# 1444-key attention: the left-over maxima as two 64-row halves beside the scores, and the turn of the maxima as a 32-column product

## The reference, cut to what matters

```python
qm = _split_heads(q @ Wq.T + bq)      # 16 heads of 8
km = _split_heads(k @ Wk.T + bk)
vm = _split_heads(v @ Wv.T + bv)
scores = jnp.einsum('bnlh,bnph->bnlp', qm, km) / np.sqrt(HEAD_DIM)
scores = jnp.where(mask, scores, MASK_FILL)
attn = jax.nn.softmax(scores, axis=-1)
out = jnp.einsum('bnlp,bnph->bnlh', attn, vm)
```

## Time and profile before

| | us |
|---|---|
| median of 3 runs | 2240.69 |
| lowest, highest | 2237.75, 2240.87 |
| profiled execution, its own time | 2244.95 |
| its span, first to last instruction | 2243.2 |

### The profile page before, as it was taken

One profiled execution on the slowest core, in us unless ns is written; L12 is line 12 of the kernel. 1 busy time (PEld: TensorE's weight loads), 2 busy tenths in 40 slices (PEclk: granted clock), 3 DMA queues, 4 the chain that ended last, 5 costly groups with the idle time before them and its releaser, 6 DMA issues. The chain is left out here.

```text
span 2243.2 us, 50114 instructions
## 1 busy us (share of the span) xinstructions
PE 1949.5 (87%) x20406; PEld 1251.7 (56%) x20406; DVE 1577.7 (70%) x3726; ACT 1326.7 (59%) x2169; POOL 551.6 (25%) x477
## 2 busy tenths in 40 slices
PE   3769999767899999999999999999996888888997
PEld 2536666544456556565565655656664565555554
DVE  4845666695888888888888888888862566664554
ACT  2635776584266666666666666666774545554444
POOL 1410323312313222132221322313212232321122
PEclk9869999676699999999999999999997778888999
DMA  4025555002213233132331322323312001103341
GB/s 154 1 72 181 185 183 156 7 27 71 102 63 124 83 107 124 66 123 86 104 124 67 123 96 93 127 68 119 119 54 66 15 8 16 31 1 60 67 77 35
DMA packets 120050, 189.71 MB, mean 85 GB/s; under 512 B 36770, under 2 KB 94090, under 8 KB 118414
## 3 DMA queue, kind: packets, MB, share of 16 engines
q1 hardware_dynamic: 119822, 186.50, 26.6%
HBM read 103.33 MB, written 11.76 MB: 51 GB/s over the span
## 5 line engine op out<-in xcount | busy, mean ns | idle before, releaser
L1619 DVE TENSOR_REDUCE b_part_max<-psum 128x1 f32<-128x482 f32 (+3 forms) x1248 | 737.6, 651 | 151.4 <-PE psum L1496 137.4
L1400 ACT ACTIVATE b_PT<-psum 128x800 f32<-128x800 f32 x768 | 618.4, 837 | 350.9 <-PE psum L1515 344.1
L1496 PE MATMUL psum<-b_KH,b_QBD 64*128 64x482 f32 (+1 forms) x1152 | 427.3, 443 | 45.8 <-DVE b_part_max L1619 42.2
L1515 PE MATMUL psum<-b_QS,b_KS 64*128 64x200 f32 x3072 | 438.5, 288 | 0.5 <-ACT b_PT L1400 0.3
L1515 PEld LDWEIGHTS psum<-b_QS,b_KS 64*128 64x128 f32 x3072 | 339.4, 186 | 16.2 <-issue 11.8
L1531 PE MATMUL psum<-b_PT,b_V 128*32 128x200 f32 x6144 | 341.1, 336 | 0.6 <-ACT b_PT L1400 0.6
L1496 PEld LDWEIGHTS psum<-b_KH,b_QBD 64*128 64x128 f32 x1152 | 196.7, 188 | 203.6 <-DVE b_part_max L1619 117.5
L1322 POOL TENSOR_TENSOR b_KL<-b_KF,b_KH 128x1444 fp32r<-128x1444 f32 x32 | 106.9, 3342 | 655.5 <-PE psum L1515 634.0
L1531 PEld LDWEIGHTS psum<-b_PT,b_V 128*32 128x32 f32 x6144 | 184.5, 109 | 110.9 <-issue 47.1
L1909 ACT ACTIVATE c_HE<-psum,C 128x400 f32<-128x400 f32 x128 | 75.7, 595 | 94.6 <-PE psum L2125 90.1
L418 POOL TENSOR_TENSOR a_rs<-a_ve,a_half 100x4 f32<-100x4 f32 x48 | 48.5, 1011 | 319.9 <-DVE a_ve L910 319.8
(11 more groups left out here) (278 smaller groups left out, 3091.5 us busy)
## 6 DMA issues: line engine op xcount, KB each, us to landing
b_KS<-b_KH SPq DMA_DIRECT2D x64, 722.0 KB
a_CT<-in_ctxt SPq DMA_DIRECT2D x32, 722.0 KB, 5.7
b_CT<-in_ctxt SPq DMA_DIRECT2D x32, 722.0 KB, 4.3
b_KS<-b_KL SPq DMA_DIRECT2D x32, 722.0 KB
a_CN<-in_ctxn SPq DMA_DIRECT2D x32, 704.0 KB
att_scratch<-b_AO SPq DMA_DIRECT2D x32, 200.0 KB, 1.9
c_G<-gates_scratch SPq DMA_DIRECT2D x4, 1600.0 KB
c_KBD<-gates_scratch SPq DMA_DIRECT2D x4, 1600.0 KB
```

What stands on the lines that cost most here:

```text
L1400: nc.scalar.activation(PT[:, kt % 2, 2 * a:2 * a + 2, :], psum[:, 2 * a:2 * a + 2, 0:TG], ACT.Exp).then_inc(sem["pt_ready"], 1)
L1496: m = mm(bank(b, D, size), QBD[rows, j % 2, tile * D:(tile + 1) * D], KH[rows, j % 2, at_:at_ + size], start=True, stop=True)
L1515: m = mm(bank(p, D, 2 * T, (s % 2) * 2 * T), KS[rows, j % 2, s, kt * D:(kt + 1) * D], QS[rows, j % 2, s * 2 * T:(s + 1) * 2 * T], start=Tr ...
L1619: v.tensor_reduce(part_max[0:rows, q, c:c + 1], bank(b, rows, CHUNKS[c][1]), AX.X, ALU.max)\
```

## The change

The left-over maxima leave phase 4 of T5, T6 and T7 and go into T2, T4 and T6 (`LEFT_TILES`). Each is now two products over 64 rows that add into the same bank: the one on half 1 in piece 0, behind the main maximum there, and the one on half 0 at the start of piece 2. The second waits for the first to be complete (`left_begun`), since both write the same bank. A ring bank is taken at piece 0; VectorE is told after the second. `QBL` is 128 columns wide instead of 64, its upper 64 zero, so that the product has the same 64 x 128 shape as its neighbours; VectorE still reduces 64 rows. The combining reduction now follows the last main maximum (T7).

The turn is a plain product with the identity in a 32-column tile of the array instead of a transpose.

In the preparation of the very first sample, the three left-over maxima come before the last main one, unsplit.

```diff
+LEFT_TILES = (2, 4, 6)
...
-        jobs += [((g, j + 1, "max", len(MAINS) + c), PHASES * (c + 5) + 4) for c in range(3)]
+        jobs += [((g, j + 1, "max", len(MAINS) + c), PHASES * kt) for c, kt in enumerate(LEFT_TILES)]
...
-        QBL = sb("QBL", [D, 2, 2 * LEFT], F32R)
+        QBL = sb("QBL", [D, 2, D], F32R)
...
+            def left_half(b, j, c, half):
+                at_, size = CHUNKS[c]
+                rows = slice(ROW * half, ROW * half + ROW)
+                return mm(bank(b, D, size), QBL[rows, j % 2, :], KH[rows, j % 2, at_:at_ + size],
+                          start=(half == 1), stop=(half == 0))
+
+            def left_rest(at, ahead, g, j, kind, i):
+                c = max_tile(i)[2]
+                pe.wait_ge(sem["left_begun"], 3 * (g * GROUP + j - 1) + c + 1)
+                left_half(RING[at % len(RING)], j, c, 0).then_inc(sem["ring_filled"], 1)
...
+                    if half is None and split:
+                        left_half(b, j, c, 1).then_inc(sem["left_begun"], 1)
+                        return
...
-                    m = nc.tensor.transpose(bank(b, QCH, D), mx[:, 0:QCH], t.ident)
+                    m = mm(bank(b, QCH, D), mx[:, 0:QCH], t.ident, start=True, stop=True, tile_position=(0, 0))
...
                         for p in range(4):
+                            if p == 2:
+                                rest(kt)
                             some(PHASES * kt + p)
...
-                    if i == MAXES - 1:
+                    if i == len(MAINS) - 1:
                         dve.wait_ge(drained, done)
                         v.tensor_reduce(mx[:, 0:QCH], part_max[:, :, :], AX.X, ALU.max, negate=True).then_inc(sem["mx_ready"], 1)
```

More of the change, by code:

```diff
@@ L95 @@
 SIGNALS = """
-att_free att_ready b_chain b_cleared consts_loaded ht_loaded kh_ready kl_ready m_turn_psum mx_ready nm_ready
+att_free att_ready b_chain b_cleared consts_loaded ht_loaded kh_ready kl_ready left_begun m_turn_psum mx_ready nm_ready
 ones_ready pen_ready0 pen_stored pt_ready pv_done q_ready qbd_ready qexp_ready quotient_ready rd_ready ring_drained
@@ L1120, in first_ring_jobs @@
     jobs = [(0, 0, "query", r) for r in range(Q_JOBS)] + [(0, 0, "key", r) for r in range(3)]
-    for i in range(MAXES):
+    for i in (*range(len(MAINS) - 1), *range(len(MAINS), MAXES), len(MAINS) - 1):
         jobs.append((0, 0, "max", i))
-        if i % 12 == 3 and i < len(MAINS):
+        if i % 12 == 3:
             jobs.append((0, 0, "value", i // 12))
@@ L1289, in _ @@
             pl.memset(KS[:, :, :, S:].bitcast(F32), 0.0)
+            pl.memset(QBL[:, :, 2 * LEFT:].bitcast(F32), 0.0)
             pl.memset(mx[:, :], 0.0).then_inc(sem["b_cleared"], 1)
@@ L1300, in spread_tiles @@
                                  K[:, K_M8:K_M8 + 8].unsqueeze(2).to_broadcast([D, 8, T]), ALU.mult)
[L1301 removed]
+                pl.tensor_tensor(QBL[:, j % 2, 0:2 * LEFT].rearrange("p (b q) -> p b q", b=2),
                                  QT[:, (n // GROUP) % 2, (j % GROUP + 1) * T - LEFT:(j % GROUP + 1) * T].unsqueeze(1).to_broadcast([D, 2, LEFT]),
@@ L1448, in by_columns, with job @@
                 return m
-            def job(at, ahead, g, j, kind, i):
+            def left_half(b, j, c, half):
[7 more added lines that the diff above has]
+                left_half(RING[at % len(RING)], j, c, 0).then_inc(sem["ring_filled"], 1)
+            def job(at, ahead, g, j, kind, i, split=False):
                 n = g * GROUP + j
@@ L1491, in job @@
                     at_, size = CHUNKS[c]
+                    if half is None and split:
+                        left_half(b, j, c, 1).then_inc(sem["left_begun"], 1)
+                        return
                     if half is None:
-                        m = mm(bank(b, 2 * LEFT, size), QBL[:, j % 2, :], KH[:, j % 2, at_:at_ + size], start=True, stop=True)
+                        m = mm(bank(b, D, size), QBL[:, j % 2, :], KH[:, j % 2, at_:at_ + size], start=True, stop=True)
                     else:
@@ L1543, in some, with rest @@
                             if where == k:
-                                job(*place(g, j, i), *what)
+                                job(*place(g, j, i), *what, split=True)
+                    def rest(kt):
+                        for i, (what, where) in enumerate(jobs):
+                            if what[2] == "max" and what[3] >= len(MAINS) and where == PHASES * kt:
+                                left_rest(*place(g, j, i), *what)
                     for kt in range(KT):
```

## The result

| us | before | changed |
|---|---|---|
| median of 20 runs each | 2241.35 | 2249.73 |
| lowest, highest | 2230.99, 2248.93 | 2245.56, 2261.51 |
| profiled execution's span | 2243.2 | 2253.5 |

The ratio is 1.0051 with a 95% interval of 1.0036 to 1.0066: the change costs 2241.35 x 0.0051 = 11.4 us (8 to 15). The two medians alone differ by 8.4. The forecast was 12.9, in a range of 2243 to 2264.

A forecast was written before the change was run, and what follows sets the result against it. The prediction took waits for a ring bank that VectorE must give back as the bound. 17 samples at +0.48 and 14 at +0.34 add 12.9 to 2240.69: 2253.6 us, own range 2246 to 2262, 8-in-10 range 2243 to 2264.

The forecast's parts named there:

- The bound: In most tiles a ring bank that VectorE must give back sets the length; a fourth job before phase 4 costs 0.57.
- T2, +0.57: In T2 the values take the left-over job's bank and start one reduction later, 2.22 instead of 1.65 us.
- T4, +0.69, and T6, +0.11: T4's values at 1.92 us (0.57 plus 0.12 for a late second half); T6's key at 1.92 instead of 1.81.
- T5, -0.52; T7, -0.37: Phase 4 loses its left-over product: T5's `weigh` starts 0.52 us earlier, T7's key 0.37 earlier.
- T8, 0: The turn as a plain product leaves T8's length the same, with bounds of -0.21 and +0.22 us.
- turn to key far from 0.2: Sign of being wrong, in T8: the time from the turn to the key product far from 0.2 us.
- With a query job, +0.34: Samples with a query job in T5, 14 of 31, become 0.34 us longer each.
- The sum: Over the 31 preparations of a next sample, 17 x 0.48 + 14 x 0.34 = 12.9 us slower.
- A: Rival: TensorE is the bound, T2 and T4 add nothing or 0.3 each; faster, 2195 or 2214 us; chance 0.12.
- B: Rival: second halves in time in T4 and T6, turn hidden in T8; about the same, 2241.5 us; chance 0.10.
- C: Rival: TensorE's wait for its own `left_begun` costs T4 and T6 0.3 each; slower, 2268 us; chance 0.12.
- D: Rival: a left-over half runs before the scores, not beside them; up to 0.2 us a tile, no separate chance.

The follow-up runs named there:

- fewer_beside: The changed kernel with one main maximum each moved from T2 and T4 into T5 and T7; loop 1045.4 us, ratio 1.0035 to the kernel before.
- unsplit: The changed kernel with each left-over maximum as one product over all 128 rows, without the wait for left_begun; loop 1048.1 us, ratio 1.0060 to the kernel before.
- t8_two: The kernel before with the turn as a product and one main maximum each moved from T10 and T11 into T8; loop 1015.4 us, ratio 0.9919.
- t8_three: The kernel before with the turn as a product and one main maximum each moved from T9, T10 and T11 into T8; loop 1015.8 us, ratio 0.9938.
- turn_only: The kernel before with only the turn made a plain product instead of a transpose; loop 1036.7 us, ratio 1.0019.

## Why the prediction was right, point by point

**The bound.** Right. The page's 87% of TensorE says otherwise; T0, a tile with four jobs ahead of its phase-4 job, decided against it. `fewer_beside` and `unsplit` show that the number of jobs before the values sets their start in the main; what TensorE has to multiply adds 0.15 and 0.11 in their T4 and nothing in T2. `t8_two` moved the same products to other tiles and won 21 us besides the turn's 1. What was argued from one row, 0.57 a job, came back as 0.56 (T2), 0.57 (T8 of `t8_three`) and 0.58 (T9).

**T2, +0.57.** Measured +0.56.

**T4, +0.69, and T6, +0.11.** +0.77 and +0.18: the mis-sized term is the lateness of the second half, 0.12 in the forecast and 0.18 or 0.19 measured. The half started as forecast, at 0.75 (1001.55 - 1000.80). It took 0.48, the length of a product that starts on an idle half, where I took the middle of 0.38 and 0.48, and that is the 0.06 missing: 0.75 + 0.48 + 0.04 for the semaphore = 1.27, against 1.09 when VectorE wanted it. The first row of a phase, not a later one, was the row to read. These are about 3 us over the loop (T4 +22.5 where 20.7 were forecast, T6 +2.1 where 1.0 was), of which T2, T5, T7 and T8 give 1.4 back.

**T5, -0.52; T7, -0.37.** -0.53 and -0.38.

**T8, 0.** -0.03. The bounds, -0.21 and +0.22, were much wider than needed; the value taken was that of a by-column job on one strip, and the key's product on the turn's strip starts 0.22 behind the turn, as worked out. But one sign of being wrong came true: "turn to key far from 0.2". The key starts 0.01 behind the turn on the other strips, and `weigh` is 0.17 longer, so the tile's end hardly moves. The sign was badly chosen, since the mechanism forecast for T8 itself lets the other strips start at once.

**With a query job, +0.34.** +0.34 and +0.33 in the two kinds of sample.

**The sum.** 12.9 for 31 samples, so 12.6 for the 30 of the loop time (17 without a query in T5, 13 with one); measured 13.9. The lower end of my own range, 2246, should have been 2247 by its terms (2240.69 + 7.3 - 1); nothing hangs on it. The whole runs agree too (11.4, with 8 to 15), but they couldn't tell 12.6 from 8; the tiles can.

**Rivals.** A (TensorE is the bound) is excluded by T2 and T4. B asked for halves in time and a hidden turn: neither was so. C was half right in its mechanism, but its sign, a second half over 0.9 after the tile's start, did not come (0.75). TensorE does wait for itself: its weight loads stand idle for 0.23 before each second half, in the view by tile of `QBL` (idle time before its instructions, and how often).

```profile
  PE psum L1456: 21.7, 93
```

These are 21.7 us of idle weight loads in all; the products themselves pause for only 0.05 before the half of T4 (1001.50 to 1001.55). Of this, what reaches the path is the lateness in T4 and T6, 0.18 or 0.19, 0.06 more than forecast; the rest lies below VectorE's wait. D does not apply: the first half starts 0.32 after T4's start, while the scores on the other half run from 0.00 to 0.70.

## What to carry to other kernels

Where jobs share a ring of banks in order, find for each job of the bound engine the one *n* places before it, and when that one is read out. This gives the price of a job in each place, and it may be nothing for the engine that looks busiest. Price every job behind the inserted one this way, not only the next. And before an order is turned round to hide a wait, ask what the old order was hiding: here `weigh` covered VectorE's latency for the next tile, and giving that up cost more than the wait it saved (shown in T2 and T9).

## What the runs showed of the hardware that was not expected

A by-column product and a product on one column strip overlap almost fully: the key's other strips start 0.01 after the turn (1013.06 and 1013.07). The transpose held them 0.21. The gain did not reach the tile's end, since the next shape waits for the last strip.

Products of the two row halves overtake each other. In T7 of the changed kernel the queue has four scores between the first and the second main maximum, but seven scores started before the second (the row x7 from 1009.94, ahead of 1010.47): three scores of the upper half ran while the lower half was still at its own four.

Whole executions of one kernel differed by up to 24 us, and the time went with the granted clock: of `turn_only`'s twelve, the shortest has 2225.26 at 0.927 and the four longest 2247.41 to 2249.31 at 0.913. The loop was granted 1.00 in the profiled executions of all kernels but the two with `weigh` first, so a loop's own rows resolve what whole runs can't. Where the clock does dip inside the loop, the length of that one tile shows it.
